# One reduction over two score banks in place of two, both banks released together, and a later place for the rotary sum

## What is computed

```python
x = x + 0.5 * ffn(layernorm(x))     # 32 experts, top 8, kept to cumulative 0.8
x = x + attn(layernorm(x))
x = x + 0.5 * ffn(layernorm(x))

# attn, 16 query heads on 4 key/value heads of 16 features
q = q * cos + rotate_half(q) * sin
k = k * cos + rotate_half(k) * sin
attn = softmax(q @ k.T * scaling, axis=-1)
out = (attn @ v) @ Wo.T
```

## Time and profile before

| | us |
|---|---|
| median of 3 runs | 2269.64 |
| runs | 2267.43 to 2271.03 |
| profiled execution, its own time | 2266.18 |
| its span in the profile | 2264.4 |
| PE busy | 2201.2 (97%) |
| DVE busy | 1597.2 (71%) |
| ACT busy | 1173.5 (52%) |
| POOL busy | 1094.3 (48%) |

### The profile page before, as it was taken

How to read it: one execution, slowest core, us unless ns; L and a number is a source line. 1 busy time by engine, 2 the same in 40 slices (tenths; PEclk the granted TensorE clock), 3 DMA queues, 4 the chain that set the end, 5 groups by cost and what they waited for, 6 DMA issues and landing times.

```text
span 2264.4 us, 47194 instructions
## 1 busy us (share of the span) xinstructions
PE 2201.2 (97%) x18794; PEld 1487.3 (66%) x18794; DVE 1597.2 (71%) x3139; ACT 1173.5 (52%) x1925; POOL 1094.3 (48%) x956
## 2 busy tenths in 40 slices
PE   3999999999999999999999999999999999999998
PEld 2888875565566565565566566666666666688887
DVE  8756679787887877877877876777777754444543
ACT  4433331566656556556556666665666656433332
POOL 1767654354444444544434443444444344466665
PEclk9999999999999999999999999999999999999999
DMA  5211121011111120111201110010110010101010
GB/s 223 81 42 36 40 58 30 20 45 32 35 31 41 25 61 24 36 37 31 48 25 46 27 50 23 20 43 18 24 52 13 20 30 20 30 27 41 21 39 20
DMA packets 157957, 88.51 MB, mean 39 GB/s; under 512 B 103588, under 2 KB 149924, under 8 KB 156968
## 3 DMA queue, kind: packets, MB, share of 16 engines
q1 hardware_dynamic: 157592, 85.45, 14.0%
q10 hardware_dynamic: 144, 0.03, 0.0%
HBM read 63.14 MB, written 11.80 MB: 33 GB/s over the span
## 4 chain that ended last, share of the span: by engine, by line
PE 91%; DVE 6%; POOL 1%; issue 1%; DMA 1%; ACT 0%; SPq 0%; POOLq 0%; DVEq 0%
PE PS L1262 44%; PE PS L1283 22%; PE PS L1295 11%; PE PS L1328 10%; DVE arena L1003 2%; PE PS L1244 1%; PE PS L1357 1%; PE PS L1307 1%; DVE arena L980 1%; DVE arena L988 1%; POOL arena L611 1%; POOL arena L616 0%; PE PS L1230 0%; DVE parts L1096 0%; DVE arena L970 0%
## 5 line engine op out<-in xcount | busy, mean ns | idle before, releaser
L1262 PE MATMUL PS<-XT,WGU 128*128 128x256 f16 x9216 | 1112.3, 273 | 5.6 <-DVE arena L980 2.3
L1262 PEld LDWEIGHTS PS<-XT,WGU 128*128 128x128 f16 x9216 | 875.9, 98 | 223.6 <-issue 121.2
L616 POOL TENSOR_TENSOR arena<-arena 128x512 f16<-128x512 f32 x384 | 450.8, 1174 | 1059.8 <-ACT arena L695 1059.8
L1003 DVE TENSOR_REDUCE arena<-PS 128x1 f32<-128x512 f32 x1024 | 657.3, 684 | 299.9 <-PE PS L1295 295.3
L711 ACT ACTIVATE arena<-PS,fac 128x512 f32<-128x512 f32 x1024 | 646.3, 684 | 263.7 <-PE PS L1307 263.2
L688 ACT ACTIVATE arena<-PS,fac 128x512 f32<-128x512 f32 x384 | 263.8, 687 | 758.3 <-PE PS L1262 758.3
L1283 PE MATMUL PS<-WD,arena 128*128 128x256 f16 x4608 | 572.8, 274 | 2.6 <-POOL arena L616 2.4
L611 POOL TENSOR_TENSOR arena<-arena 128x512 f32<-128x512 f32 x384 | 501.5, 1306 | 72.8 <-DVE arena L988 68.7
L1283 PEld LDWEIGHTS PS<-WD,arena 128*128 128x128 f16 x4608 | 430.8, 98 | 151.4 <-issue 95.5
L980 DVE SCALAR_TENSOR_TENSOR arena<-arena,PS 128x512 f32<-128x512 f32 x384 | 261.1, 680 | 253.2 <-ACT arena L688 252.2
L1295 PE MATMUL PS<-arena 48*128 48x512 f16 x1024 | 318.8, 382 | 18.2 <-DVE arena L1003 13.5
(11 more groups left out here) (119 smaller groups left out, 732.2 us busy)
## 6 DMA issues: line engine op xcount, KB each, us to landing
arena<-ce_scratch SPq DMA_DIRECT2D x256, 128.0 KB, 3.2
arena<-wgu SPq DMA_DIRECT2D x4, 1536.0 KB, 13.0
arena<-q_scratch SPq DMA_DIRECT2D x192, 32.0 KB
arena<-ktab_c SPq DMA_DIRECT2D x16, 256.0 KB, 3.7
q_scratch<-arena SPq DMA_DIRECT2D x32, 128.0 KB, 1.8
out<-X SPq DMA_DIRECT2D x8, 512.0 KB, 3.0
X<-wd SPq DMA_DIRECT2D x2, 1536.0 KB, 23.1
X<-x SPq DMA_DIRECT2D x1, 3072.0 KB, 11.7
```

Of the source, the lines that this page charges most:

```text
L616: pool.tensor_tensor(hs[1][:, d % HS, :], tw[d % 2], hs[0][:, d % HS, :], ALU.subtract).then_inc(lo_done, 1)
L1003: dve.tensor_reduce(mx[:, half * REP * QT + c:half * REP * QT + c + 1], PS[:, B_MAX + half, :], AX_X, ALU.max).then_inc(max_taken, 1)
L1262: ins = pe.matmul(PS[:, b, j * HALF_G:(j + 1) * HALF_G], WGU[w][:, kt, part * CHUNKS + c + j, :], XT[r][:, k % 2, kt, half * HALF_G:(half ...
```

## The change

- `maximum(f)` waits for both banks and takes one maximum over 1024 columns that lie in both. It leaves one column instead of two, and adds one to `max_taken` instead of two.
- `score_max(f, half)` waits for `max_taken >= f` for either half.
- `mx` keeps its 64 columns, now as two buffers of 32 for units in turn. The first maximum of a unit waits until the unit before the last has been split (`ml_lo >= u - 1`).
- `max_rows`, its buffer `mxm`, its semaphore and `unit_ends` go. `max_rows_high` and `max_rows_low` read the maxima directly.
- On DVE `rope_sum` moves from ahead of position 1 to behind position 2 (or 1). `turn_max_rows` stands one slot earlier.
- On POOL `max_rows_low` moves from behind `weigh(d + 1)` to directly behind `low(d)`. On SP `rows(u)` stands one slot earlier.

```diff
+        def maxima(u):
+            return mx[:, u % 2 * REP * QT:(u % 2 + 1) * REP * QT]
...
-                    if d == ROWS_AT[u] + 2:
+                    if d == ROWS_AT[u] + 1:
                         rows(u)
...
                 if 0 <= d < SLOTS:
                     low(d)
+                if d - 1 in ROWS_AT:
+                    max_rows_low(ROWS_AT.index(d - 1))
...
-                act.wait_ge(mx_max, u + 1)
+                act.wait_ge(max_taken, FILLS * (u + 1))
...
                 c = (2 * i + par) * QT + t
-                for half in range(2):
-                    dve.wait_ge(max_ready, 2 * f + half + 1)
-                    dve.tensor_reduce(mx[:, half * REP * QT + c:half * REP * QT + c + 1], PS[:, B_MAX + half, :], AX_X,
-                                      ALU.max).then_inc(max_taken, 1)
-            def max_rows(u):
-
-                dve.wait_ge(max_taken, 2 * FILLS * (u + 1))
-                if u:
-                    dve.wait_ge(ml_lo, u)
-                dve.tensor_tensor(mxm[:, :], mx[:, 0:REP * QT], mx[:, REP * QT:], ALU.max).then_inc(mx_max, 1)
-                dve.wait_ge(mx_max, u + 1)
+                u = f // FILLS
+                if u > 1 and f % FILLS == 0:
+                    dve.wait_ge(ml_lo, u - 1)
+                dve.wait_ge(max_ready, 2 * f + 2)
+                dve.tensor_reduce(maxima(u)[:, c:c + 1], PS[:, B_MAX:B_MAX + 2, :].rearrange("p b n -> p (b n)"), AX_X,
+                                  ALU.max).then_inc(max_taken, 1)
...
-                if s - 1 in join_slots(k):
-                    rope_sum(k - 1, join_slots(k).index(s - 1))
...
                 if (d, 2) in VISIT:
-                    unit_ends(VISIT[d, 1])
                     visit(VISIT[d, 2])
-                if d - 2 in ROWS_AT:
-                    turn_max_rows(ROWS_AT.index(d - 2))
+                if s - 1 in join_slots(k):
+                    rope_sum(k - 1, join_slots(k).index(s - 1))
+                if d - 1 in ROWS_AT:
+                    turn_max_rows(ROWS_AT.index(d - 1))
...
                 if f:
-                    pe.wait_ge(max_taken, 2 * f - 1 + half)
+                    pe.wait_ge(max_taken, f)
```

More of the change, by code:

```diff
@@ L238, in build @@
         pad = sb("pad", [P, 1])
-        mxm = sb("mxm", [P, REP * QT])
         parts = sb("parts", [P, 8])
@@ L372, in build @@
         rows_T, rows_out = sem("rows_T"), sem("rows_out")
-        o_inv, mx_max, ml_hi, ml_lo = sem("o_inv"), sem("mx_max"), sem("ml_hi"), sem("ml_lo")
+        o_inv, ml_hi, ml_lo = sem("o_inv"), sem("ml_hi"), sem("ml_lo")
         o_rows, o_norm, o_hi, o_lo, o_cols, yo_done, xo_done = (
@@ L632, in max_rows_low @@
                 pool.wait_ge(ml_hi, 2 * u + 2)
-                pool.tensor_tensor(ml[:, REP * QT:], mxm[:, :], ml[:, 0:REP * QT], ALU.subtract).then_inc(ml_lo, 1)
+                pool.tensor_tensor(ml[:, REP * QT:], maxima(u), ml[:, 0:REP * QT], ALU.subtract).then_inc(ml_lo, 1)
             inverse_roots(0)
@@ L653, in _ @@
                         rows_low(norm_of_group(k + 1))
-                if d - 1 in ROWS_AT:
-                    max_rows_low(ROWS_AT.index(d - 1))
                 if d in OUT_AT:
@@ L733, in max_rows_high @@
             def max_rows_high(u):
-                act.wait_ge(mx_max, u + 1)
+                act.wait_ge(max_taken, FILLS * (u + 1))
                 if u:
                     act.wait_ge(rows_T, u)
-                act.activation(ml[:, 0:REP * QT], mxm[:, :], ACT.Copy, scale=1 / M_UNIT).then_inc(ml_hi, 1)
-                act.activation(mxm[:, :], mxm[:, :], ACT.Copy, scale=1 / M_UNIT).then_inc(ml_hi, 1)
+                act.activation(ml[:, 0:REP * QT], maxima(u), ACT.Copy, scale=1 / M_UNIT).then_inc(ml_hi, 1)
+                act.activation(maxima(u), maxima(u), ACT.Copy, scale=1 / M_UNIT).then_inc(ml_hi, 1)
             rows_high(0)
@@ L1028, in visit @@
                         turn_outputs(q // QT)
[L1031 to L1035, removed]
             def turn_outputs(hv):
@@ L1147, in _ @@
                     product(d + 1)
-                if (d, 0) in VISIT:
-                    unit_ends(VISIT[d, 0])
-                if s - 1 in join_slots(k):
-                    rope_sum(k - 1, join_slots(k).index(s - 1))
                 if d == -1 or d == 0:
@@ L1194, in _ @@
                     event(d, 0)
[L1195 to L1198, removed]
         @block.tensor
```

## The result

| | before | after |
|---|---|---|
| median of 6 runs each, us | 2268.81 | 2277.49 |
| range, us | 2266.34 to 2271.03 | 2276.61 to 2279.13 |
| profiled execution, span, us | 2264.4 | 2275.4 |

The changed kernel is slower: the ratio is 1.004, 95% interval 1.0027 to 1.0053. The difference of the medians is 8.7 us; 9.7 was forecast. The median of before from the first three runs, 2269.64, lay somewhat high, so the sum on it, 2279.3, is 1.8 us over what was measured. The two profiled executions, 2266.18 and 2277.15, lie 11.0 apart: that of before was faster than all six runs of before, that of after stands in the middle of its own.

A forecast was written before the change was run, and what follows sets the result against it. PE was taken to set the end, busy 97% of the span, so the change could only touch its holds. Terms summed to +9.7 us: 2275.9 from the profiled 2266.18, 2279.3 from the median 2269.64; range 2268 to 2296.

The forecast's parts named there:

- 20 third visits at 0.15: Third score fills of slots like 218: PE's hold grows from 0.15 to 0.466 us, 20 x 0.316 = +6.3 us.
- slots 67 to 69 and 75: Three-visit slots where routing or norm pieces make DVE the bound: about 0.6 us a slot less shorter maxima, +1.7 us.
- first and second visits behind long DVE work: 18 held fills like slot 253, behind norm and dense sum: each hold grows by 0.25 to 0.316 us, +4.9 us.
- pairs of neighbouring holds: Holds on PE at neighbouring visits: the time only moves from one visit to the next, zero in the sum.
- four new holds: Four visits with a DVE backlog just under what holds PE today become holds of 0.2 us: +0.8 us.
- rotary sum, slots 83, 183, 203 and what follows: Moved behind the maxima, holds of 2.07, 1.21 and 2.06 us fall; some returns at next visits: net -3.1, small holds -0.1.
- first unit's rows: PE's 3.39 us wait for the first unit's rows goes when they come a slot earlier: -3.4 us; later units no gain.
- The joined wait: Idle DVE starts 0.226 us later, ends 0.158 later with a 1.220 us maximum; held PE loses 0.226 more at release.
- The 26 ns margin: 120 second visits with DVE idle keep 0.184 - 0.158 = 0.026 us of margin before PE is held: cost zero.
- The long maximum: Rival: crossing banks makes the joined maximum longer than 1.244 us; 2291 us at 1.288, 2316 at 1.368; chance 0.12.
- Absorbed: Rival: held PE lets DVE catch up, so the 4.9, 0.8 and 1.7 us fall away: +2.3, 2272 us; chance 0.20.
- relief: Rival: DVE's 0.068 us savings add up over backlogs of five or more maxima, long holds halve: -7.4, 2262 us; chance 0.10.

The follow-up runs named there:

- The two single-edit runs: Kernel before with only PE's fills waiting for both maxima: 2283.92 us against 2267.92; with only DVE's first maximum waiting for both banks: 2283.13 against 2267.92.
- both good edits and two maxima: Kernel before with rotary sum behind the slot's last maxima, and rows and POOL's split moved earlier, two maxima a visit: 2256.38 us against 2267.99.
- 2250.37 in two pieces: Kernel before with rotary sum and rows moved, two maxima a visit, second visit's maxima ahead of product in three-visit slots: 2250.37 us against 2268.77.
- 2261.41 in one: Changed kernel with the second visit's joined maximum between gated and product in slots of three visits: 2261.41 us against 2267.92 for the kernel before.
- a reordering that the holds pointed at: Second visit's maxima put ahead of product in three-visit slots; on the kernel before with rotary sum and rows moved, 2250.37 us against 2256.38 without it.

## Why the prediction was right

The holds of each fill, before and after, by the prediction's own steps:

| step | forecast, us | measured in the traces, us |
|---|---|---|
| 20 third visits at 0.15 | +6.3 | +6.4 |
| 5 third visits at 0.22 | +1.2 | +1.5 |
| 5 other third visits | +1.6 | +1.1 |
| slots 67 to 69 and 75 | +1.7 | +3.2 |
| first and second visits behind long DVE work | +4.9 | +4.4 |
| pairs of neighbouring holds (slots 108, 132, 180) | 0 | -1.1 |
| four new holds | +0.8 | +0.6 |
| second visits with DVE idle, and other small new holds | 0 | +2.5 |
| rotary sum, slots 83, 183, 203 and what follows | -3.2 | -4.0 |
| first unit's rows | -3.4 | -3.3 |
| sum (the joins of maxima, -0.2 in the forecast, are not in it) | +9.9 | +11.3 |

The mechanism and the direction were right, and the large terms came out. That the sum is as near as it is, is in part luck: the terms that measured higher than forecast did so by 4.5 us in all, those that measured lower by 3.1, and only 1.4 is left. And the forecast of 9.7 lies between the 8.7 of the medians and the 11.0 of the two profiled executions.

**The joined wait** was right in mechanism and size: 0.226 for the release, 0.158 for the start, 1.22 for the maximum. The twenty third visits read 0.461 to 0.473 in all but two slots for a forecast 0.466. The two single-edit runs show both terms apart.

**The 26 ns margin** was 33 ns, and 111 of the 120 second visits kept it. (The prediction gives 1.94 us between two visits that nothing holds; its own rows and all others have 1.95. Its margin was worked out from the rows, so nothing hangs on it.) But two parts of that step were wrong, and both are waits on a second semaphore.

The first is on DVE. 21 second visits behind a norm or similar piece are held 0.035 each, 0.7 us in all. I had read the 0.07 by which DVE started late at them in the kernel before as work not yet done, covered by the later second fill. It isn't work. DVE sits idle and still starts 0.07 later than elsewhere. The changed kernel in slot 82, DVE then PE:

```profile
437.71 0.16 DVE L897 TENSOR_TENSOR rstd<-nw,rs 128x4 f32<-128x4 f32 x1
438.42 1.23 DVE L1007 TENSOR_REDUCE arena<-PS 128x1 f32<-128x1024 f32 x1 [0.55 <-PE PS L1277]
```

```profile
437.71 0.39 PE L1277 MATMUL PS<-arena 48*128 48x512 f16 x1
```

0.71 behind the first fill, not 0.64, though DVE's last instruction ended at 437.87. In these slots the program waits on a semaphore of that last instruction too. The traces bear out that this second wait is the 0.07, though no run took it away: in the kernel before, all 29 maxima that DVE starts idle and 0.07 late have a second wait, and none of those that start on time has one, whichever instruction came last, norm pieces among them. It needn't be a wait on DVE's own work. In the changed kernel the new wait on `ml_lo`, which POOL sets, stands ahead of a unit's first maximum, and in slots 146 and 248, where it is the only second wait, DVE starts 0.07 late too. The prediction set that wait at nothing, and it costs nothing only because those visits have the room behind them.

The second is on PE. Nine second visits are held 0.055 each, and so are the first visits of slots 164 and 204 and one more second visit. At these fills PE waits for `q_in` or `rows_in` as well as for the maximum: they are the first fill of a unit, or the fill of the visit that begins a unit's exponentials. The changed kernel in slot 222, DVE then PE:

```profile
1394.61 1.22 DVE L1007 TENSOR_REDUCE arena<-PS 128x1 f32<-128x1024 f32 x1 [1.54 <-PE PS L1277]
```

```profile
1395.98 0.37 PE L1277 MATMUL PS<-arena 48*128 48x512 f16 x1
```

The maximum ends 0.147 ahead of the fill, by the trace's ns; a released fill with one wait starts 0.057 behind it. The same 0.09 makes the hold of 0.55 in slot 218, and the one in slot 74. In the kernel before these fills waited only for the maximum of their own bank, which ended 0.69 us or more ahead, so the longer way didn't show. Again no run took the second wait away. Three more visits are held 0.12 to 0.58, slot 149 among them, where both second waits meet. None of these was in the sum.

**Slots 67 to 69** were sized at half. DVE's own chain there was right, but two of its routing instructions became 1.15 and 0.98 us long, where they took 0.17 and 0.18 before. DVE, then POOL, of the changed kernel:

```profile
336.62 1.15 DVE L923 TENSOR_SCALAR r<-r 128x4 f32<-128x4 f32 x1
...
345.09 0.98 DVE L935 TENSOR_SCALAR XN<-keep 128x32 f32<-128x32 f32 x1
```

```profile
336.59 1.15 POOL L618 TENSOR_TENSOR arena<-arena 128x512 f16<-128x512 f32 x1 [3.19 <-ACT arena L697]
```

The shift laid each under a POOL instruction that starts 0.02 or 0.21 before it and ends within 0.04 of it; the second one is the same L618 at 344.88. The other 15 executions of each line took 0.17 to 0.20. That POOL's work is the cause is read from this coincidence, in two traces; no run moved POOL's instruction alone. That is 1.8 us on a stretch where DVE is the bound, against a miss of 1.5. The prediction counted DVE's work at its length of before, and by these rows that length depends on what POOL does beside it.

**The rotary sum** gained 0.8 more than forecast, most likely by the same effect, the other way: in slots 83 and 203 it ran beside POOL in its old place (1.13), and alone in the new one (0.67), so less came back at the next visit. The hold of slot 132 fell by 1.2, where I had set such pairs at zero; why it fell wasn't followed up.

**The first unit's rows** gained their wait, but the step had no term for the clock. In the changed kernel the low stretch isn't gone, it stands at 349 us, behind the 2.1 us pause in slot 68, so the profile of after doesn't show this gain. The run with the rows alone has a low stretch elsewhere; only the trace with both good edits and two maxima has none before its end.

**The rivals.** The long maximum (2291, 2316) fell with the 1221 ns. Absorbed named three terms that wouldn't grow; they grew by 4.4, 0.6 and 3.2 for a forecast 4.9, 0.8 and 1.7. It and relief fell with the parts that add, too: +17.7 for the joining alone is even more than the +16.5 (9.7 + 3.2 + 3.4 + 0.2) of my sum. The rule of the Trainium skill in "Perfetto Trace Analysis", section "Optimizing Scalar/DVE Operations", that work of an unsaturated engine which causes bubbles elsewhere may end sooner in pieces, agrees with these runs: 2250.37 in two pieces, 2261.41 in one.

## What to carry to other kernels

When a producer refills a buffer that a reader hands back, ask when the first piece is handed back, not how much work the reader does: joining two short reductions saved 0.07 us of DVE a visit and cost PE some 0.3 at most holds, 18 us in all. Work out the margin in the tightest place to the nanosecond, and separately for the places where the program waits on two semaphores: a whole class of visits falls together, and those fall first. And when a change bundles edits, run each alone: two of these three were worth 11 us, and a reordering that the holds pointed at was worth 6 more.

## What the runs showed of the hardware

- Several traces show TensorE's granted clock at its lower level for 3.4 us (0.59 in the mean of 403 to 407 us of the kernel before), or for twice that, behind a pause of PE. The pauses ahead of these stretches were 1.1 to 4 us. Not each such pause has one: the hold of the rotary sum in slot 203, 1.6 us, has one with the rows alone and none in the kernel before.
- The runs of the kernel before lie in groups near 2266.5, 2268.2 and 2270.6, and their mean granted clocks, 0.999, 0.998 and 0.997, fall in that order. Those of the kernel with sum and rows moved, whose trace has no low stretch before its end, lie within 0.5 us. That the groups are numbers of low stretches (up to 1.7 us each) fits, but wasn't shown: no trace of the slower groups was kept.
- A maximum over 1024 columns in two PSUM banks costs 1221 ns, and one over as many SBUF columns 1222: crossing the banks costs nothing that shows.
- A DVE write of one column ahead of a maximum moved it by 0.009 us, a DVE copy of one column by 0.07, though they show 0.06 and 0.15 us of their own.
- A DVE instruction on four columns took 1.15 us in place of 0.17 while POOL worked on 512.
- Where the program waits on a second semaphore, an idle DVE started its maximum 0.07 us later (0.49 in place of 0.42 behind the first fill, in 29 of 29 cases of the kernel before), and PE its fill 0.147 in place of 0.057 behind the end of the maximum that released it.
